# A state-space block beside a routed mixture of experts: the first batch's B, C and step-size projections moved into three PSUM banks of their own, between placement chunks 3 and 4

## What is computed

```
xn = layernorm(x)                                   # no gain, no offset
out = x + mamba(xn) + moe(xn)

mamba(v):   xs, gate = split(v @ in_w.T + in_b)      # 256 + 256 columns
            xc = silu(causal_conv4(xs) + conv_b)
            B, C = split(xc @ bc_w.T + bc_b)         # 16 + 16 columns
            dt = softplus(xc @ dt_w.T + dt_b)        # 256 columns
            h = h * exp(dt * A) + dt * B * xc        # per token, 256 x 16 states
            y = (sum_n h * C + D * xc) * silu(gate)
            return layernorm(y @ out_w.T + out_b + v) * ln_g + ln_b
moe(v):     logits = silu(v @ rw1 + rb1) @ rw2 + rb2   # 8 experts, the best 2 of each token
            return v + sum over the 2 of weight * (silu(v @ we1[e] + be1[e]) @ we2[e] + be2[e])
```

## Time and profile before

| what | value |
|---|---|
| median of 3 runs (lowest, highest) | 936.59 us (936.52, 938.70) |
| the profiled execution, its own time | 936.73 us |
| its span, first to last instruction | 934.3 us |
| mean granted TensorE clock | 0.961 of full speed |
| busy: PE, DVE, ACT, POOL | 787.8, 787.8, 664.3, 601.2 us |
| stage 3 begins (first `inputs` on VectorE) | 132.34 us |

### The profile page before, as it was taken

One profiled execution on the slowest core, in us unless ns is written; L12 is line 12 of the kernel. 1 busy time (PEld: TensorE's weight loads), 2 busy tenths in 40 slices (PEclk: granted clock), 3 DMA queues, 4 the chain that ended last, 5 costly groups with the idle time before them and its releaser, 6 DMA issues.

```text
span 934.3 us, 14382 instructions
## 1 busy us (share of the span) xinstructions
PE 787.8 (84%) x4533; PEld 634.1 (68%) x4533; DVE 787.8 (84%) x774; ACT 664.3 (71%) x1134; POOL 601.2 (64%) x384
## 2 busy tenths in 40 slices
PE   3993669978998899888989899889989997899852
PEld 2662647857776677677876777677768786778741
DVE  6818839798889968998899698989899889989993
ACT  1433668777688768876886878886878788869930
POOL 3571515757477757876767756884787487758861
PEclk9996989999999999999999999999999999999985
DMA  9939437568566865797668775786577667877731
GB/s 298 389 142 345 173 109 242 138 205 272 180 209 199 255 222 187 209 278 217 212 203 241 238 239 152 233 273 203 185 219 256 215 210 222 244 226 228 227 90 22
DMA packets 81927, 201.00 MB, mean 215 GB/s; under 512 B 7936, under 2 KB 41216, under 8 KB 81728
## 3 DMA queue, kind: packets, MB, share of 16 engines
q1 hardware_dynamic: 61424, 171.46, 53.4%
q0 software_dynamic: 19168, 26.59, 14.9%
q10 hardware_dynamic: 1264, 2.05, 0.7%
HBM read 174.38 MB, written 26.61 MB: 215 GB/s over the span
## 4 chain that ended last, share of the span: by engine, by line
DVE 36%; PE 27%; ACT 10%; issue 9%; DMA 6%; SPq 1%; POOL 1%; DVEq 0%; ACTq 0%; POOLq 0%
DVE ps_drive L935 13%; PE ps_up L1229 11%; DVE ring L942 9%; DVE ps_drive L928 7%; PE ps_yx L1243 6%; DMA bc_scratch<-sp 6%; PE ps_fr L1160 5%; ACT L787 3%; DVE xx L909 2%; ACT da L760 2%; PE ps_fr L1185 1%; PE ps_up L1223 1%; SPq L524 1%; DMA out<-yo,sid 1%; PE ps_up L1288 1%
## 5 line engine op out<-in xcount | busy, mean ns | idle before, releaser
L592 POOL TENSOR_TENSOR y<-y,ring 128x1024 f32<-128x1024 f32 x126 | 325.5, 2583 | 59.1 <-ACT y L751 51.8
L935 DVE TENSOR_TENSOR_SCAN ps_drive<-da,ps_drive 128x1024 f32<-128x1024 f32 x128 | 293.7, 2295 | 41.5 <-ACT da L760 37.8
L1229 PEld LDWEIGHTS ps_up<-xgt,w1s 128*128 128x128 f32 x2272 | 284.7, 197 | 17.9 <-issue 9.6
L1229 PE MATMUL ps_up<-xgt,w1s 128*128 128x128 f32 x2272 | 284.6, 280 | 0.0
L1243 PE MATMUL ps_yx<-w,ht 128*128 x1136 | 270.7, 382 | 0.0
L1243 PEld LDWEIGHTS ps_yx<-w,ht 128*128 128x128 f32 x1136 | 206.4, 192 | 28.8 <-issue 5.0
L581 POOL DMA_INDIRECT out<-yo,sid x71 | 117.9, 1660 | 147.0 <-ACT yo L802 107.6
L787 ACT ACT_TABLE_LOAD x143 | 183.5, 1283 | 2.5
L760 ACT ACTIVATE da<-gd,col 128x511 f32<-128x511 f32 x256 | 168.3, 710 | 0.0
L928 DVE TENSOR_TENSOR ps_drive<-ps_u,rep 128x1024 f32<-128x1024 f32 x128 | 157.4, 1229 | 9.5 <-DVE ring L942 0.5
L942 DVE TENSOR_TENSOR ring<-ps_drive,rep 128x1024 f32<-128x1024 f32 x128 | 156.5, 1223 | 3.9
(11 more groups left out here) (161 smaller groups left out, 724.1 us busy)
## 6 DMA issues: line engine op xcount, KB each, us to landing
w1s<-in_we SPq DMA_DIRECT2D x71, 1024.0 KB, 7.3
rep<-bc_scratch SPq DMA_DIRECT2D x128, 512.0 KB, 4.4
w<-in_we SPq DMA_DIRECT2D x8, 1024.0 KB, 11.9
w<-in_x SPq DMA_DIRECT2D x8, 512.0 KB, 11.0
xn_scratch<-da SPq DMA_DIRECT2D x8, 512.0 KB, 7.2
out<-w POOLq DMA_DIRECT2D x8, 512.0 KB, 6.2
xnt_scratch<-xx SPq DMA_DIRECT2D x8, 512.0 KB, 5.7
xx<-xnt_scratch SPq DMA_DIRECT2D x8, 512.0 KB, 3.3
```

Of the source, the lines that this page charges most:

```text
L592: pool.tensor_tensor(y[:, :, :], y[:, :, :], ring[:, g % RING, :, :], ALU.add).then_inc(s_sum, 1)
L935: dve.tensor_tensor_scan(states, da[:, g % DECAYS, :, :].rearrange("p k l -> p (k l)"), states, 0.0, ALU.mult, ALU.add).then_inc(s_scanned, 1)
L1229: mm = pe.matmul(bank[:, c * P:(c + 1) * P], w1s[:, q, k, at:at + P], xgt[:, k, :], start=False, stop=(c == 3 and k == KD - 1))
```

## The change

The three projections of batch 0 no longer use bank `fr`. They go into three banks that are unused at that time: `up1` (B and C), `yx` (dt, m = 0) and `tr0` (dt, m = 1; the trace calls it `ps_drive`). TensorE issues all three in a row after chunk 3, once `conv_act` is done, with no wait between them. ScalarE reads B and C between `weights_in(4)` and `weights_in(5)`, and the two dt halves where it did before. New semaphores `s_first_mm` and `s_first_read` take the place of the bank's counters, the table `uses` loses three entries, and TensorE waits for all three reads before `turn_x(0)`.

```diff
-        uses = [("in", 0, 0), ("in", 0, 1), ("bc", 0, 0), ("dt", 0, 0), ("dt", 0, 1)]
+        uses = [("in", 0, 0), ("in", 0, 1)]
+        FIRST = ("up1", "yx", "tr0")
...
                 def store_bc(b):
-                    sync.wait_ge(s_fr_read, front["bc", b, 0] + 1)
+                    if b == 0:
+                        sync.wait_ge(s_first_read, 1)
+                    else:
+                        sync.wait_ge(s_fr_read, front["bc", b, 0] + 1)
...
+                def first_bc():
+                    act.wait_ge(s_first_mm, 1)
+                    act.wait_ge(s_link, 1)
+                    act.wait_ge(s_bias_step, 3)
+                    act.activation(bcs, psum[FIRST[0]][0:NBC, :], ACT.Identity,
+                                   bias=col[0:NBC, C_BCB:C_BCB + 1]).then_inc(s_first_read, 1)
+
+                def first_dt(m):
+                    act.wait_ge(s_first_mm, m + 2)
+                    if m == 1:
+                        act.wait_ge(s_bc_stored, 16)
+                    act.activation(sp[:, m, :], psum[FIRST[m + 1]][:, :], ACT.Abs,
+                                   bias=col[:, C_DTB + m:C_DTB + m + 1]).then_inc(s_softplus, 1)
+                    act.activation(xsv[:, m, :], psum[FIRST[m + 1]][:, :], ACT.Identity,
+                                   bias=col[:, C_DTB + m:C_DTB + m + 1]).then_inc(s_first_read, 1)
+
...
                     if n == 4:
                         conv_act(0)
+                    if n == 5:
+                        first_bc()
                     weights_in(n)
-                bc_in(0, 2)
-                dt_in(0, 0, 3)
-                dt_in(0, 1, 4)
+                for m in range(KD):
+                    first_dt(m)
...
+                def first(bank, at, rows_out):
+                    for k in range(KD):
+                        mm = pe.matmul(psum[bank][0:rows_out, :], wm[:, k, at:at + rows_out], xc[:, k, :],
+                                       start=(k == 0), stop=(k == KD - 1))
+                    mm.then_inc(s_first_mm, 1)
+
                 for n in range(NCH):
+                    if n == 4:
+                        pe.wait_ge(s_conv, KD)
+                        first(FIRST[0], W_BC, NBC)
+                        for m in range(KD):
+                            first(FIRST[m + 1], W_DT + m * P, P)
                     chunk(n)
-                proj_bc(0, 2)
-                proj_dt(0, 3)
-                proj_dt(1, 4)
+                pe.wait_ge(s_first_read, 3)
```

More of the change, by code:

```diff
@@ L431, in build @@
         s_expert = sem("s_expert")
+        s_first_mm = sem("s_first_mm")
+        s_first_read = sem("s_first_read")
         s_tile_onehot = sem("s_tile_onehot")
@@ L713, in conv_act @@
                         act.activation(xc[:, m, :], xc[:, m, :], ACT.Silu).then_inc(s_conv, 1)
+                def first_bc():
[12 more added lines that the diff above has]
+                                   bias=col[:, C_DTB + m:C_DTB + m + 1]).then_inc(s_first_read, 1)
                 def bc_in(b, f):
                     act.wait_ge(s_fr_ready, f + 1)
[L717 to L721, removed]
+                    act.wait_ge(s_dt, b)
                     act.activation(bcs, psum["fr"][0:NBC, :], ACT.Identity,
```

## The result

| kernel | median | lowest to highest | executions |
|---|---|---|---|
| before | 938.91 us | 932.55 to 948.35 | 22 |
| changed | 932.50 us | 929.72 to 937.38 | 22 |

The ratio is 0.9942 (95% interval 0.9926 to 0.9959), a gain of 5.4 us (3.8 to 6.9) on 938. It is not the quotient of the two medians, which is 0.9932 (6.4 us) and lies in the same interval. On the 936.59 us shown ahead of the prediction the ratio makes 931.2; both that and the median of 932.5 lie in the predicted 928.3 to 933.4. In the narrower range given for the forecast itself, 929.5 to 932, lies the 931.2 but not the median. Single executions of the changed kernel spread over 8 us, and the traced one of the changed kernel, at 937.38 us and a span of 935.0, is the slowest of its 22. Its end therefore says nothing on the gain; its start does, and its loop shows what the spread is made of.

A forecast was written before the change was run, and what follows sets the result against it. No single engine bounds the kernel; stage 3's start, set by the softplus chain, passes to the end. A 6.1 us shift from 936.73 gives 930.6, less 0.14 for the median: 930.5; 8-in-10 range 928.3 to 933.4.

The forecast's parts named there:

- The sign and the end: Whole kernel: faster by 6.1 us, to 930.5 us; faster was given 0.85, a gain of 5 to 7 0.58.
- That the chain ran through exp and ln, with the gather behind them: Before stage 3: the softplus (exp, ln) is last in the kernel before; the gathered tokens have 5.7 us of slack.
- The projections: TensorE between chunks 3 and 4: 1.98 us each, chunk 4 then 2.25, so the last placement comes 0.83 later.
- ScalarE's reads and the store: B and C's read costs nothing, their store lands before the second dt pair, exp and ln end at 123.96.
- I take 4.7 as the nearest: First tile's gather, now crossing SP's loads: lands 4.7 us after issue, like the gather at 127.24; copy_x(0) at 126.1.
- the rival of 8.3: Loads crowd the gather out: 8.3 us to land, gain 2.5, time 934.1; chance 0.12, shared with a low clock's 1.6.
- The rival time of 928.8: First gather as quick as alone, 3.0 us: copied at 124.4, gain 7.8 us; chance 0.17.
- The clock after the gap: TensorE idle from 119.2 to 125.6: low clock again hidden behind ScalarE's decays, counted as nothing; 1.6 us if not.
- VectorE's first scan: Start of stage 3: scan begins at 129.2, 6.9 us earlier, behind a new wait of 1.4 on ScalarE.
- Rigid shift: Stage 3 to the end: nothing is fixed in time, so what its first instructions gain, 6.1 us, the end gains.
- rival S: Set up after the prediction, for the loop: the shifted start makes later batches slower, 713 us or more; no chance given.
- waits of a batch: In the loop: transfers meeting at other moments can move single waits; start's gain given back, 936 to 937, chance 0.07.

The follow-up runs named there:

- e2: Changed kernel with the projections back after chunk 7 and B and C read after the last weights_in; three banks kept: 933.25 us against 938.19 before.
- e3: Changed kernel with only B and C projected before chunk 4; dt halves after chunk 7, sharing bank yx: 934.26 us against 938.19 before.
- e1: Changed kernel, but SP issues one broadcast load, then waits for the first gather before the other two and xtok: 930.42 us against 938.19 before.
- e7: Changed kernel, but SP issues one broadcast load and xtok, then waits for the first gather before the other two: 932.59 us against 937.89 before.
- e8: Changed kernel with B and C in a buffer of their own instead of the second half of sp: 919.32 us against 937.89 before.
- e4: Changed kernel with 16 extra ScalarE copies between the first tile's turn and copy_x(0): 941.60 us against 938.19 before.
- e10: The kernel before with B and C in a buffer of their own and nothing else: 924.31 us against 936.23 before.
- e6: The changed kernel run once more, unaltered, beside the kernel before: ratio 0.9942 (0.9903 to 0.9981).

## Why the prediction was right or wrong

*The sign and the end: right, in part by luck.* Faster, and within the wide range, while the median of 932.5 lies above the forecast's own 929.5 to 932. A gain of 6.1 was forecast, 5.4 (3.8 to 6.9) measured. But the agreement is better than the working: the shift that the forecast rests on was 4.2, and 1.9 of the 6.1 were not there.

*That the chain ran through exp and ln, with the gather behind them: right.* In e2 and e3, which shorten only that chain, `copy_x(0)` came earlier by 2.3 and 3.5 us, where 2.1 and 3.3 were expected.

*The projections: the mechanism right, the term too large.* 1.98 each was the pace with waits between; unbroken they took 5.37 for three, and chunk 4 took 2.18, not 2.25. The placements came 0.24 later instead of 0.83, just under the lower bound of 0.3.

*ScalarE's reads and the store: right.* The store was issued at 107.72 and the second dt pair did not wait for it. exp and ln ended at 123.2 where 123.96 was said.

*"I take 4.7 as the nearest": the step that failed.* It sized the wait for the moved gather, the term on which the whole shift of 6.1 hangs, at 4.7 us; 6.8 was measured. The gather at 127.24 was issued 2 to 4 us behind SP's loads. The moved one was issued within a microsecond of three of them. I had read "crossed by the same loads" as the same condition, and it was not: by e1 and e7 the landing goes with the number of loads issued around the gather, and by the later gathers of changed, e2 and before it goes with the order in time, which no run tried by itself. The landing took 6.8 and 6.9 in two traces (and 6.8 in e8), between the forecast and the rival of 8.3. It cost 2.1 us of the 6.1; the placements gave 0.6 back, and the turn, at the low clock, took another 0.3. That is the 1.8 by which the copy came later than forecast. The rival time of 928.8, for a gather as quick as alone, was not the change's; e1 reached a landing of 3.3 only by holding the loads back. With the rule of queues in turn (the Trainium skill, "DMA: Bandwidth & Descriptors", section "Queues, rings and completion order") the stretch in which each queue had 47% agrees. The 3.5 us before it, in which the loads' queue had 80% and more and the gather's next to nothing, do not, unless the gather's packets were not there yet.

*The clock after the gap: right but for 0.3 us.* The low stretch lay at about 121 to 131 and the two `up` groups took 3.23 and 1.95, hidden behind ScalarE's decays; `hidden` did not wait. But the first tile's turn fell into it and took 0.66, where 0.41 had been counted.

*VectorE's first scan: the mechanism right, the wait mis-sized.* It did wait for a decay, but 4.15 us and not 1.4, since `inputs` came 0.8 earlier than said and the copy 1.8 later.

*Rigid shift: right at the point, and not seen in the one trace.* The forecast said that it would be wrong "if the first `hidden` moves by 6 and the end does not". It moved by 4.3, and the traced end came 0.7 later. That test was badly chosen: it set two single executions against each other, whose loops differ by up to 6 us. The 93.6 us in twelve traces, and e4 against e1, show the shift passed on; how much of it the loop gives back in a single trace stays open (rival S, above). What I had called "waits of a batch" that can move is real, and larger than thought: one boundary's wait for a store, with the clock behind it, decides up to 2 us. The range was meant for a median; a single execution of the changed kernel falls outside it at 937.

## What to carry to other kernels

When a chain is shortened, what was ready early and merely queued behind it becomes the next end, and its latency must be taken for the new moment: ask what else is being issued then, and how much of it is still to move. Holding three loads back for one small gather brought the copy 3.6 us forward and took the gain from 5.4 to 8.9 us, with intervals that still touch. Where two executions of one kernel differ by more than the change is worth, compare intervals between two named instructions, and judge the end by medians. And look at buffers that share a place with something being stored: one wait in each of seven boundaries (0.2 to 4.6 us, often 2 to 4), and the clock that it cost, were worth more than twice the whole change (e10: 12.8 against 5.4). How much of that is the wait and how much the clock was split for one boundary only.

## What the runs showed of the hardware that had not been expected

- A small indirect gather on GpSimd's queue moved next to nothing from its issue at 120.27 to about 125.5 while SP's broadcast loads ran, then took half of the engines; with nothing around it, its first packets moved about 1.5 us after the issue. Landed in 3.0, 3.3, 5.7 and 6.8 us with none, one, two and four loads of 512 KB around it.
- At the boundaries between batches, TensorE idle for 4.08, 4.22, 4.44 and 4.61 us before a group (changed, e7, e6 twice): that group of sixteen took 3.62. Idle for up to 1.86: 1.95, the full pace, each time. Between 1.87 and 3.69 both occurred: 2.66 after 1.87 in e6, 3.05 after 2.20 in e2, 3.62 after 2.96 in the changed kernel, and 1.95 after 3.69 in e3.
- The stages ahead of the loop vary as well: the index table was written at 118.86 and 119.43 in two traces of before, and at 119.09 and 121.19 in two of the changed kernel.
